# Layer 3's keys, values and products: biases by TensorE, banks emptied by ScalarE, masking moved into layer 2's expert loop

## The chip, the cores and the metric

The kernel runs on one core of a Trainium2 chip. The metric is device time in microseconds (us): the median of several executions. A core has five engines that run their own instruction streams in order and wait for one another by semaphores: TensorE (PE in the rows; its weight loads are PEld), VectorE (DVE), ScalarE (ACT), GpSimd (POOL) and SyncE (SP, which here only starts DMA transfers).

## The reference

A model of four layers, each an attention and a feed-forward part, over `x` (8 batches of 256 tokens of 256 numbers) and a context `ctx_1024` of the same shape. The change touches two neighbouring parts.

Layer 2's feed-forward part is a mixture of 8 experts with 2 chosen for each token:

```python
logits = jnp.einsum('bsd,de->bse', x, Wg) + bg
probs = jax.nn.softmax(logits / TEMP, axis=-1)
vals, idx = jax.lax.top_k(probs, K)
...
h = jax.nn.gelu(jnp.einsum('bsd,edh->besh', x, W1) + b1[None, :, None, :], approximate=False)
out = jnp.einsum('besh,ehd->besd', h, W2) + b2[None, :, None, :]
y = jnp.einsum('bse,besd->bsd', gates, out)
```

Layer 3's attention has 16 heads of 16 numbers and no softmax; its keys and values come from the context alone, not from `x`:

```python
K = _split_heads(_linear(k, wk_w, wk_b))
V = _split_heads(_linear(v, wv_w, wv_b))
score = jnp.einsum('bhqd,bhkd->bhqk', Q, K) / dk
attn = jnp.where(mask, -jnp.inf, score)
ctx = jnp.einsum('bhqk,bhkd->bhqd', attn, V)
```

Without a softmax, the context product of a head is the query times the small matrix K^T V of that head.

## The kernel before, in words

The program is a row of stages, one after the other on each engine: `setup, l0, e0, p1, f1, p2, e2, x3, f3`. `e2` is layer 2's mixture of experts (class `Experts`; `e0` is layer 0's, the same class), `x3` layer 3's attention, `f3` its feed-forward part, `p2` layer 2's attention. Stages are parted by a fence at which each engine waits for the others. Nothing is scheduled by a planner: each engine's order is the order in which its method of the stage (`pe`, `dv`, `ac`, `po`, `sp`) issues.

What layer 3's attention needs of the context does not depend on `x`, so it is computed inside stage `e2`, through hooks that `Experts` calls on the objects in its tuple `beside`. For each batch b (8 of them):

- `keys_pe(b)`: TensorE multiplies the context of the batch (256 tokens, in `ctxT`) with `wk` into one PSUM bank and with `wv` into another, 8 float32 matmuls of 256 columns; the profile shows each float32 matmul as two instructions (L2044, x16 a batch);
- `keys_dv(b)`: VectorE adds the bias row and writes `Ks` and `Vs` to SBUF (L2078, 128x512, twice a batch);
- in `amid_pe(b)`: TensorE forms the product K^T V, two blocks of 128x128, in bank 6 (L2064, x8 in the profile);
- in `amid_dv(b)`: VectorE multiplies it with the block mask `blk` (heads of 16, and the factor 1/4) and writes `As[b]`, over the part of `ctxT` that is no longer needed (L2089).

Of stage `e2` itself these steps stand around it, in this order on TensorE: transposes of the normalised tokens (`Norm.pe`, L283), the gate's logits (L957, L962), one pair of matmuls that counts the tokens of each expert (L912, L913), a list of places (`slots_pe`, L936, 32 matmuls in four groups of 8), and then the expert loop over 39 tiles of 128 tokens: transpose (`turn_pe`, L982), up (`up_pe`, L997) and down (`down_pe`, L947). VectorE's routing between the logits and the end of the list is one chain (`select`, `route`, `slots_dv`, `listed_dv`). `slots_dv` builds `values`, whose second half is `inblk` times the lane number `pid` (L1113), and `onehot` (L1115, 32 instructions; after each 8 the semaphore `seated` lets TensorE's next group go). When the list is done, SP starts to load the expert weights (four buffers) and POOL gathers the tokens. TensorE's order before was:

```python
self.norm.pe(t, lambda g: self.logits_pe(t, g))
# keys_pe(0), the counting pair, keys_pe(1), slots_pe
for n in range(9):
    # amid_pe(n): product of batch n, then keys_pe(n + 2)
self.turn_pe(t, 0)
```

`step_dv(v, i)` is a hook that VectorE calls once for each tile i of the expert loop.

## Time and profile before

| | |
|---|---|
| Median of 3 runs | 1799.55 us (1798.6 to 1801.32) |
| The profiled execution: its own time | 1807.56 us |
| Its span in the trace | 1805.8 us |
| Mean TensorE clock granted | 0.941 of full |
| Busy: TensorE, VectorE, ScalarE, GpSimd | 87%, 59%, 50%, 22% of the span |
| Stage `e2` in the trace, from its fence | 1404 us to about 1632 us |

The table's clock is the mean over the span of what the chip granted TensorE; a stretch has either 1.00 (2.4 GHz) or 0.50 (1.2 GHz). Times of the trace count from the start of the span of that one execution, which was 8 us slower than the median; a difference worked out in it is subtracted from the median.

### The profile page before, as it was taken

How to read it: one execution, taken by the hardware profiler on the slowest of the kernel's cores; microseconds unless marked ns; L12 is line 12 of the kernel's file. 1: busy time of each engine (PE TensorE's matmuls, PEld its weight loads, DVE VectorE, ACT ScalarE, POOL GpSimd, SP SyncE). 2: the span in 40 equal slices, each digit the busy share in tenths (PEclk: the TensorE clock that was granted, in tenths of full speed). 3: DMA queues.
4: the chain of work that ended last, by engine and by line, in shares of the span. 5: the costliest groups of instructions: out<-in, count | busy, mean ns of one | idle time of the engine just before them, and what ended most of it. 6: DMA issues, size and time to landing. Idle time of an engine off the chain costs nothing.

```text
span 1805.8 us, 27818 instructions
## 1 busy us (share of the span) xinstructions
PE 1565.6 (87%) x9882; PEld 1188.7 (66%) x9890; DVE 1058.7 (59%) x2954; ACT 906.8 (50%) x2034; POOL 390.6 (22%) x488
## 2 busy tenths in 40 slices
PE   7999965999489999999858699999999689995566
PEld 5777645999357766667535666677766378994444
DVE  7767744111556667666567755555555644225887
ACT  4888831333156666666539455555555102333366
POOL 1000012222232333332240100000000115543734
PEclk9999977999799999999968899999999889997879
DMA  5000047998300000000000200000000149993001
GB/s 167 1 2 1 2 140 291 325 328 280 120 6 7 7 7 7 7 1 1 1 1 1 82 12 7 7 7 7 1 1 1 59 147 309 359 337 104 1 12 36
DMA packets 57496, 143.92 MB, mean 80 GB/s; under 512 B 8208, under 2 KB 35088, under 8 KB 51088
## 3 DMA queue, kind: packets, MB, share of 16 engines
q1 hardware_dynamic: 49296, 123.80, 19.5%
q0 software_dynamic: 5952, 16.26, 2.7%
q10 hardware_dynamic: 2112, 2.10, 0.4%
q8 instruction: 79, 1.29, 0.3%
q14 instruction: 57, 0.47, 0.1%
HBM read 127.72 MB, written 14.42 MB: 79 GB/s over the span
## 4 chain that ended last, share of the span: by engine, by line
PE 70%; DVE 16%; ACT 6%; issue 4%; POOL 3%; DMA 2%; POOLq 1%; SPq 0%; DVEq 0%; ACTq 0%
PE bank L997 8%; PE bank L1425 8%; PE bank L947 8%; PE bank L1479 7%; PE bank L1492 6%; PE bank L1466 5%; PE bank L1429 5%; PE bank L1409 3%; PE bank L669 3%; PE bank L1831 2%; PE bank L685 2%; PE bank L700 2%; ACT p1f L1547 1%; PE bank L2044 1%; PE bank L606 1%
## 5 line engine op out<-in xcount | busy, mean ns | idle before, releaser
L1676 DVE TENSOR_REDUCE small<-bank 128x1 f32<-128x512 f32 x128 | 82.4, 686 | 108.7 <-PE bank L1479 108.7
L1672 DVE CUSTOM_DVE_ANT_0 p1f<-bank,p1f 128x512 f32<-128x512 f32 x128 | 83.2, 687 | 80.9 <-PE bank L1479 80.9
L1550 ACT ACTIVATE p2f<-bank,small 128x512 f32<-128x512 f32 x128 | 86.9, 684 | 86.2 <-DVE small L1676 86.2
L399 POOL TENSOR_SCALAR rs<-mv 128x4 f32<-128x4 f32 x16 | 3.6, 226 | 569.8 <-DVEq L229 554.1
L741 ACT ACTIVATE l<-l,small 128x256 f32<-128x256 f32 x256 | 108.9, 502 | 32.5 <-DVE small L807 32.1
L1547 ACT ACTIVATE p1f<-p1f,small 128x512 f32<-128x512 f32 x128 | 91.2, 714 | 67.5 <-DVE small L1672 67.2
L1016 ACT ACTIVATE e2a<-bank,WB 128x128 f32<-128x128 f32 x156 | 44.6, 369 | 158.8 <-PE bank L997 99.7
L807 DVE CUSTOM_DVE_ANT_0 l<-bank,small 128x256 f32<-128x256 f32 x256 | 90.8, 421 | 13.4 <-PE bank L685 12.5
L1425 PE MATMUL bank<-WA,HT 128*128 128x256 f32 x384 | 94.1, 389 | 4.9 <-DVE p1f L1617 4.9
L1561 ACT ACTIVATE p2f<-bank 128x512 f32<-128x512 f32 x128 | 75.2, 598 | 40.5 <-PE bank L1466 39.0
L1016 ACT ACTIVATE e0a<-bank,WB 128x128 f32<-128x128 f32 x128 | 36.6, 368 | 96.6 <-PE bank L997 96.6
L206 POOL TENSOR_TENSOR small<-small,nhalf 128x8 f32<-128x8 f32 x48 | 80.3, 1672 | 4.0
L1561 ACT ACTIVATE p1f<-bank 128x512 f32<-128x512 f32 x128 | 74.1, 589 | 13.2 <-PE bank L1466 13.2
L1425 PEld LDWEIGHTS bank<-WA,HT 128*128 128x128 f32 x384 | 71.0, 195 | 14.7 <-DVE p1f L1617 5.6
L997 PEld LDWEIGHTS bank<-e2a,WB 128*128 128x128 f32 x624 | 75.6, 192 | 5.6 <-issue 3.7
L997 PE MATMUL bank<-e2a,WB 128*128 128x128 f32 x624 | 76.2, 275 | 2.9 <-DVE e2a L1191 2.9
L1466 PE MATMUL bank<-ident,p1f 128*128 128x128 f32 x512 | 75.0, 275 | 3.4 <-ACT p1f L1561 2.2
L1466 PEld LDWEIGHTS bank<-ident,p2f 128*128 128x128 f32 x512 | 60.8, 141 | 23.6 <-ACT p2f L1561 13.3
L1466 PEld LDWEIGHTS bank<-ident,p1f 128*128 128x128 f32 x512 | 59.8, 141 | 24.5 <-ACT p1f L1561 17.4
L1479 PE MATMUL bank<-p1f 64*128 64x512 f32 x256 | 73.1, 641 | 2.1 <-ACT p1f L1528 2.1
L1466 PE MATMUL bank<-ident,p2f 128*128 128x128 f32 x512 | 74.7, 275 | 0.0
L1479 PE MATMUL bank<-p2f 64*128 64x512 f32 x256 | 73.6, 641 | 1.1 <-ACT p2f L1550 1.1
(414 smaller groups left out, 3822.0 us busy)
## 6 DMA issues: line engine op xcount, KB each, us to landing
WB<-in_L2pack SPq DMA_DIRECT2D x39, 514.0 KB
WB<-in_L2pack SPq DMA_DIRECT2D x39, 512.0 KB
WB<-in_L0pack SPq DMA_DIRECT2D x16, 1028.0 KB
WB<-in_L0pack SPq DMA_DIRECT2D x16, 1024.0 KB
e0a<-in_L0pack SPq DMA_DIRECT2D x7, 1028.0 KB
e0a<-in_L0pack SPq DMA_DIRECT2D x7, 1024.0 KB
e2a<-given_y SPq DMA_DIRECT2D x8, 512.0 KB, 6.5
WB<-in_ctx ACTq DMA_DIRECT2D x4, 512.0 KB
```

What stands on the lines that cost most here:

```text
L741: ins = a.e.activation(P[:, h * 256:(h + 1) * 256], P[:, h * 256:(h + 1) * 256], ACT.Exp, scale=-1.0, bias=self.mx[:, m + h:m + h + 1])
L807: ins = v.e.tensor_tensor_reduce(P[:, h * 256:(h + 1) * 256], k.bank(x)[:, h * 256:(h + 1) * 256], self.causal[:, h, :], -1.0, 3.0e38, ALU ...
L947: ins = t.e.matmul(y[:, 0:256], self.gb[i % 2][:, c, :], w[:, self.n1 + c * 256:self.n1 + (c + 1) * 256], start=c == 0, stop=c == nf - 1)
L997: ins = t.e.matmul(bk[:, j * 128:(j + 1) * 128], w[:, c * ff + ft * 128:c * ff + ft * 128 + 128], self.xT[i % 2][:, c, :], start=c == 0, s ...
L1425: ins = t.e.matmul(bk[:, i * 256:(i + 1) * 256], x[:, c, i * 128:(i + 1) * 128], w[:, c, at], start=c == 0, stop=c == 1)
L1429: ins = t.e.matmul(bk[:, i * 256:(i + 1) * 256], w[:, c, hg * 256 + i * 128:hg * 256 + (i + 1) * 128], x[:, c, :], start=c == 0, stop=c == 1)
L1466: ins = t.e.transpose(T[:, j * 128:(j + 1) * 128], self.P[u % 4][:, j * 128:(j + 1) * 128], k.ident[:, :])
L1479: t.e.matmul(k.bank(i % 2), self.Q[g % 2][rows, c, a * 128:(a + 1) * 128], self.K[g % 2][rows, c, :], start=True, stop=True).then_inc(self ...
L1492: ins = t.e.matmul(k.bank(4)[64 * o:64 * o + 64, c * 256:c * 256 + 256], self.V[g % 2][:, j, h * 64:(h + 1) * 64], self.PT[n % 2][o][:, j, ...
L1547: ins = a.e.activation(P, P, ACT.Exp, scale=-1.0, bias=self.mx[:, m:m + 1], accum_out=self.sm[:, m:m + 1])
L1550: ins = a.e.activation(P, k.bank(x), ACT.Exp, bias=self.mx[:, m:m + 1], accum_out=self.sm[:, m:m + 1])
L1561: a.e.activation(self.PT[u // 4 % 2][o][:, :, h * 128:(h + 1) * 128], k.bank(2 + u % 2).rearrange("p (k n) -> p k n", k=4), ACT.Copy).then ...
```

## The change

Five things change, all but one within stage `e2`.

1. **Biases.** `split_po`, run by GpSimd in stage `p2`, splits the two bias rows into three bfloat16 parts (10 instructions on 3 partitions, with rows `big`, `mid`, `low`). `keys_pe` starts each of its four accumulation groups with a bfloat16 matmul of a 3-row matrix of ones with these parts (L2082 in the changed kernel, 256 columns): 4 more matmuls a batch, 32 in all.
2. **Banks.** ScalarE instead of VectorE empties the key and value banks (`keys_ac`, L2091) and the product's bank (`amid_ac`, L2122), as plain copies.
3. **Mask.** VectorE multiplies `As` with `blk` later, in SBUF, one batch in each of the expert loop's tiles 2 to 9 (`step_dv`, L2134).
4. **Order on TensorE.** `keys_pe(0)` goes ahead of the stage's transposes and writes banks 6 and 7; `amid_pe(n)` is now keys of batch n+1, then product of batch n; number 0 stands ahead of the counting pair, 1 to 3 between the pair and `slots_pe`, 4 to 7 behind it. A group of keys waits only for its own bank pair to be empty.
5. **`values`.** ScalarE instead of VectorE multiplies `inblk` by `pid`, in `e0` as in `e2` (L1018 for L1113); `slots_pe` waits for it (`laned`), and ScalarE for `inblk` (`parted`).

```diff
@@ Experts.pe
+        for other in self.beside:
+            other.lead_pe(t)
         self.norm.pe(t, lambda g: self.logits_pe(t, g))
         for other in self.beside:
-            other.first_pe(t)
+            other.amid_pe(t, 0)
         bk, n = k.bank(7), self.n
         t.wait_ge(self.routing, self.SELECTED)
         ...
-        for other in self.beside:
-            other.next_pe(t)
+        for n in range(1, 4):
+            for other in self.beside:
+                other.amid_pe(t, n)
         self.slots_pe(t)
-        for n in range(9):
+        for n in range(4, 8):
             for other in self.beside:
                 other.amid_pe(t, n)
@@ slots_pe
+            if n == 0:
+                t.wait_ge(self.laned, 1)
@@ Experts.ac
         a.e.activation(self.first_gelu, k.nhalf[:, 0:1], ACT.Gelu)
+        for n in range(2):
+            for other in self.beside:
+                other.amid_ac(a, n)
+        a.wait_ge(self.parted, 1)
+        a.e.activation(self.values[:, :, 1, :], self.inblk, ACT.Copy, scale=self.pid).then_inc(self.laned.sem, 1)
+        for n in range(2, 8):
+            for other in self.beside:
+                other.amid_ac(a, n)
@@ slots_dv
-        e.tensor_scalar(self.values[:, :, 1, :], self.inblk, self.pid, None, ALU.mult)
@@ Layer3Attention
+    def halves(self, b):
+        first = 6 if b == 0 else 0 if b % 2 else 2
+        return self.k.bank(first), self.k.bank(first + 1)
     def keys_pe(self, t, b):
         k, lo = self.k, b * 256
         t.wait_ge(*self.ready_w)
+        t.wait_ge(self.split, 1)
+        if b > 2:
+            t.wait_ge(self.kb, b - 1)
+            t.wait_ge(self.vb, b - 1)
+        for h, (bk, w, flag) in enumerate(zip(self.halves(b), (self.wk, self.wv), (self.km, self.vm))):
             for a in range(2):
+                o = bk[:, a * 256:(a + 1) * 256]
+                t.e.matmul(o, k.onesbb[0:3, :], self.parts[:, h * 256:(h + 1) * 256], start=True, stop=False)
                 for c in range(2):
+                    ins = t.e.matmul(o, k.ctxT[:, c, lo + a * 128:lo + (a + 1) * 128], w[:, c, :], start=False, stop=c == 1)
             ins.then_inc(flag.sem, 1)
+    def keys_ac(self, a, b):
+        for bk, dst, done, flag in zip(self.halves(b), (self.Ks, self.Vs), (self.km, self.vm), (self.kb, self.vb)):
+            a.wait_ge(done, b + 1)
+            a.wait_ge(self.am, b - 1)
+            a.e.activation(dst[b % 2], bk.rearrange("p (a n) -> p a n", a=2), ACT.Copy).then_inc(flag.sem, 1)
     def amid_pe(self, t, n):
+        if b + 1 < 8:
+            self.keys_pe(t, b + 1)
+        K, V = self.Ks[b % 2], self.Vs[b % 2]
+        t.wait_ge(self.kb, b + 1)
+        t.wait_ge(self.vb, b + 1)
+        t.wait_ge(self.ac6, b)
         ...
+        if b == 7:
+            t.wait_ge(self.ac6, 8)
+    def amid_ac(self, a, n):
+        b = n
+        if b + 1 < 8:
+            self.keys_ac(a, b + 1)
+        a.wait_ge(self.am, b + 1)
+        a.e.activation(self.As[b], self.k.bank(6)[:, 0:256], ACT.Copy).then_inc(self.ac6.sem, 1)
@@ step_dv
+        elif i < 10:
+            A = self.As[i - 2].rearrange("p (c n) -> p c n", c=2)
+            v.wait_ge(self.ac6, i - 1)
+            v.e.tensor_tensor(A, A, ... blk ..., ALU.mult).then_inc(self.ad.sem, 1)
```

What moves on the engines. In these rows a float32 matmul counts once; `e2a` is the stage's own arena (the normalised tokens, `Ks`, `Vs`, `values`), `WA` the weights of layer 3 and the bias parts, `onesbb` the ones.

TensorE at the start of stage `e2`; the last row of stage `p2` stands first. Before:

```order
L1409 MATMUL bank7<-WB 128x256 x8
L283 MATMUL bank0<-ident,e2a 128x128 x4
L283 MATMUL bank1<-ident,e2a 128x128 x4
L283 MATMUL bank2<-ident,e2a 128x128 x4
L283 MATMUL bank3<-ident,e2a 128x128 x4
L957 MATMUL bank4<-HT,gates 8x512 x2
```

Now:

```order
L1422 MATMUL bank7<-WB 128x256 x8
L2082 MATMUL bank6<-WA,onesbb 128x256
L2084 MATMUL bank6<-WA,ctxT 128x256 x2
...
L2082 MATMUL bank7<-WA,onesbb 128x256
L2084 MATMUL bank7<-WA,ctxT 128x256 x2
...
L283 MATMUL bank0<-ident,e2a 128x128 x4
L283 MATMUL bank1<-ident,e2a 128x128 x4
```

A whole group of keys and values, with its four bias matmuls, now stands between the fence and the first transpose.

TensorE from the last logits to the first work behind the list of places. Before:

```order
L962 MATMUL bank7<-ident,e2a 128x8 x8
L2044 MATMUL bank0<-WA,ctxT 128x256 x4
L2044 MATMUL bank1<-WA,ctxT 128x256 x4
L912 MATMUL bank7<-e2a,trib 128x256
L913 MATMUL bank7<-e2a,onesbb 128x256
L2044 MATMUL bank2<-WA,ctxT 128x256 x4
L2044 MATMUL bank3<-WA,ctxT 128x256 x4
L936 MATMUL bank5<-e2a,HT 128x78 x32
L2064 MATMUL bank6<-e2a 128x128 x4
```

Now:

```order
L968 MATMUL bank7<-ident,e2a 128x8 x8
L2082 MATMUL bank0<-WA,onesbb 128x256
L2084 MATMUL bank0<-WA,ctxT 128x256 x2
...
L2111 MATMUL bank6<-e2a 128x128 x4
L915 MATMUL bank7<-e2a,trib 128x256
L916 MATMUL bank7<-e2a,onesbb 128x256
L2082 MATMUL bank2<-WA,onesbb 128x256
L2084 MATMUL bank2<-WA,ctxT 128x256 x2
...
L942 MATMUL bank5<-e2a,HT 128x78 x32
```

Ahead of the counting pair one group of keys and one product stand where one group of keys stood; between the pair and the list three groups and three products stand where one group stood; behind the list three groups and four products are left of six and eight.

ScalarE from the exponential to the first Gelu of the loop. Before:

```order
L1006 ACTIVATE e2a<-e2a 128x128
L1007 ACT_TABLE_LOAD
L1007 ACTIVATE e2a<-nhalf 128x1
L1016 ACTIVATE e2a<-bank0,WB 128x128 x4
```

Now:

```order
L1012 ACTIVATE e2a<-e2a 128x128
L1013 ACT_TABLE_LOAD
L1013 ACTIVATE e2a<-nhalf 128x1
L2091 ACTIVATE e2a<-bank0 128x512
L2091 ACTIVATE e2a<-bank1 128x512
L2122 ACTIVATE ctxT<-bank6 128x256
...
L1018 ACTIVATE e2a<-e2a,small 128x32x39
...
L1030 ACTIVATE e2a<-bank0,WB 128x128 x4
```

Between them stand now 14 bank copies of 512 columns, 8 of 256, and the multiplication for `values` after the first two products. Two more copies of 512 (batch 0) stand ahead, behind the first copy of the transposed tokens (L383).

## Rows read from the trace of the kernel before

**Rows 1.** The page, busy time of each engine over the span.
```profile
PE 1565.6 (87%) x9882; PEld 1188.7 (66%) x9890; DVE 1058.7 (59%) x2954; ACT 906.8 (50%) x2034; POOL 390.6 (22%) x488
```

**Rows 2.** Busy time by stretch; after the engines TensorE's clock, DMA share, GB/s.
```profile
1445.41:1480.47 35.06, 31.12 (x161) 27.73 (x160) 18.33 (x45) 0.00 (x0) 3.03 (x3) 0.88 0.44 162
1505.08:1620.00 114.92, 114.92 (x802) 108.52 (x801) 33.59 (x72) 34.31 (x120) 63.58 (x61) 1.00 0.96 346
1406.25:1412.75 6.50, 5.61 (x19) 3.65 (x20) 5.76 (x17) 1.20 (x2) 3.27 (x5) 0.50 0.78 247
1437.00:1453.75 16.75, 8.23 (x49) 6.83 (x50) 15.40 (x63) 0.00 (x0) 3.03 (x3) 0.50 0.35 114
1445.40:1463.40 18.00, 15.10 (x70) 13.42 (x70) 11.38 (x33) 0.00 (x0) 3.03 (x3) 0.76 0.85 310
897.75:900.75 3.00, 3.00 (x16) 1.50 (x14) 0.00 (x0) 0.00 (x0) 0.00 (x0) 0.50 0.00 0
```

**Rows 3.** Timeline of TensorE: start, duration, what, idle time before it and releaser.
```profile
1407.14 3.65 PE L283 MATMUL bank<-ident,e2a 128*128 128x128 f32 x16 [5.25 <-DVE e2a L332]
...
1422.90 3.72 PE L2044 MATMUL bank<-WA,ctxT 128*128 128x256 f32 x16
1427.97 0.28 PE L912 MATMUL bank<-e2a,trib 128*128 128x256 bf16 x1 [1.35 <-DVE e2a L1067]
1428.09 0.27 PE L913 MATMUL bank<-e2a,onesbb 128*128 128x256 bf16 x1
1428.20 3.62 PE L2044 MATMUL bank<-WA,ctxT 128*128 128x256 f32 x16
1440.82 0.70 PE L936 MATMUL bank<-e2a,HT 128*128 128x78 bf16 x8 [9.00 <-DVE HT L1115]
...
1444.71 0.70 PE L936 MATMUL bank<-e2a,HT 128*128 128x78 bf16 x8 [0.60 <-DVE HT L1115]
...
1480.47 0.44 PE L982 MATMUL bank<-ident,e2a 128*128 128x128 f32 x2 [0.52 <-DVE ctxT L2089]
```

**Rows 4.** The chain that ended last, behind the list of places: start, duration, what.
```profile
1448.32 2.05 PE bank L2064 x8
1450.37 5.28 PE bank L2044 x16
1455.65 0.89 PE bank L2064 x8
1456.55 3.46 PE bank L2044 x16
```

**Rows 5.** Timeline of VectorE in the routing.
```profile
1434.14 0.42 DVE L1094 TENSOR_TENSOR e2a<-e2a 128x256 f32<-128x256 f32 x1
...
1438.92 0.54 DVE L1113 TENSOR_SCALAR e2a<-e2a,small 128x1248 bf16<-128x1248 bf16 x1
1439.37 5.29 DVE L1115 TENSOR_SCALAR HT<-e2a 128x128 bf16<-128x128 bf16 x32
...
1446.89 2.48 DVE L2078 TENSOR_TENSOR e2a<-bank,rows 128x512 f32<-128x512 f32 x4
```

**Rows 6.** Timeline of ScalarE in the same stage.
```profile
1408.35 0.60 ACT L383 ACTIVATE HT<-bank 128x512 f32<-128x512 f32 x1 [10.22 <-PE bank L283]
...
1483.58 1.14 ACT L1016 ACTIVATE e2a<-bank,WB 128x128 f32<-128x128 f32 x4 [57.51 <-PE bank L997]
```

**Rows 7.** The expert loop, timeline of VectorE and of TensorE.
```profile
1500.43 0.42 DVE L1191 COPY e2a<-bank 128x256 f32<-128x256 f32 x1
...
1501.32 1.95 PE L997 MATMUL bank<-e2a,WB 128*128 128x128 f32 x16
```

**Rows 8.** Timeline of TensorE at the end of stage p1, before the clock's 0.50 above.
```profile
895.68 1.14 PE L1466 MATMUL bank<-ident,p1f 128*128 128x128 f32 x8 [1.89 <-ACT p1f L1561]
```

**Rows 9.** Timeline of VectorE, layer 0's routing (stage e0).
```profile
277.16 0.32 DVE L1113 TENSOR_SCALAR e0a<-e0a,small 128x368 bf16<-128x368 bf16 x1
```

**Rows 10.** Timeline of GpSimd: the idle time is its whole stage p2 behind the norm.
```profile
1404.22 0.23 POOL L399 TENSOR_SCALAR rs<-mv 128x4 f32<-128x4 f32 x1 [381.04 <-DVEq L229]
```

More of the change, by code:

```diff
@@ L898, in __init__ @@
         self.routing = f("e_routing", 3)
+        self.parted, self.laned = f("e_parted", 1), f("e_laned", 1)
         self.xt_t, self.xt_d = f("e_xt_t", nt), f("e_xt_d", nt)
@@ L1017, in ac, with behind_ac @@
                                    bias=w[:, 2 * self.ff + ft:2 * self.ff + ft + 1]).then_inc(self.gel.sem, 1)
+    def behind_ac(self, a, g):
+        self.logits_ac(a, g)
+        for other in self.beside:
+            other.norm_ac(a, g)
     def over(self, x):
@@ L1148, in dv @@
         self.listed_dv(v)
-        for other in self.beside:
-            other.first_dv(v)
         self.worth(v)
-        for n in range(9):
-            for other in self.beside:
-                other.amid_dv(v, n)
         self.turn_dv(v, 0)
@@ L1716, in po @@
         self.norm.po(q)
+        if self.which == 2:
+            self.after_po(q)
         if self.which == 1:
@@ L1745, in ahead_sp, with lead_pe, norm_ac @@
         pass
-    def first_pe(self, t):
+    def lead_pe(self, t):
         pass
-    def next_pe(self, t):
-        pass
-    def first_dv(self, v):
+    def norm_ac(self, a, g):
         pass
@@ L1757, in amid_pe @@
         pass
-    def amid_dv(self, v, n):
+    def amid_ac(self, a, n):
         pass
@@ L2006, in __init__ @@
         self.kb, self.vb, self.qb = f("x3_kb", 8), f("x3_vb", 8), f("x3_qb", 8)
+        self.split, self.ac6 = f("x3_split", 1), f("x3_ac", 8)
         self.am, self.ad, self.cm, self.ca = f("x3_am", 8), f("x3_ad", 8), f("x3_cm", 8), f("x3_ca", 8)
@@ L2027, in weights, with splits, split_po @@
         (self.wq, self.wk, self.wv, self.wo), self.ready_w = W, ready
+    def splits(self, free):
+        self.big, self.mid, self.low, self.parts = (free[0:3, i * 256:(i + 1) * 256].bitcast(BF16) for i in range(4))
+        self.rest = free[0:3, 1024:1536]
+    def split_po(self, g):
+        k, e, rest = self.k, g.e, self.rest
+        at = ROWS["bk"][0]
+        both, one = k.rows[0:3, at:at + 512], k.ident[0:3, :]
+        g.chain(e.tensor_copy(self.big, both))
+        g.chain(e.tensor_tensor(rest, both, self.big, ALU.subtract))
+        g.chain(e.tensor_copy(self.mid, rest))
+        g.chain(e.tensor_tensor(rest, rest, self.mid, ALU.subtract))
+        g.chain(e.tensor_copy(self.low, rest))
+        for x, j in ((self.big, 0), (self.mid, 1), (self.low, 2)):
+            g.chain(e.tensor_scalar(x, x, one[:, j:j + 1], None, ALU.mult))
+        g.chain(e.tensor_tensor(self.mid, self.mid, self.low, ALU.add))
+        e.tensor_tensor(self.parts, self.big, self.mid, ALU.add).then_inc(self.split.sem, 1)
     def free(self, t, key):
@@ L2038, in keys_pe @@
         t.wait_ge(*self.ready_w)
-        for h, w, flag, was in ((0, self.wk, self.km, self.kb), (1, self.wv, self.vm, self.vb)):
-            bk = k.bank(2 * (b % 2) + h)
-            t.wait_ge(was, b - 1)
+        t.wait_ge(self.split, 1)
[3 more added lines that the diff above has]
+        for h, (bk, w, flag) in enumerate(zip(self.halves(b), (self.wk, self.wv), (self.km, self.vm))):
             for a in range(2):
+                o = bk[:, a * 256:(a + 1) * 256]
+                t.e.matmul(o, k.onesbb[0:3, :], self.parts[:, h * 256:(h + 1) * 256], start=True, stop=False)
@@ L2049, in first_pe, with lead_pe, norm_ac @@
+    def lead_pe(self, t):
         self.keys_pe(t, 0)
-    def next_pe(self, t):
-        self.keys_pe(t, 1)
+    def norm_ac(self, a, g):
+        if g == 0:
+            self.keys_ac(a, 0)
     def amid_pe(self, t, n):
         k, b = self.k, n
-        if b < 8:
-            K, V = self.Ks[b % 2], self.Vs[b % 2]
-            t.wait_ge(self.ad, b)
-            t.wait_ge(self.kb, b + 1)
-            t.wait_ge(self.vb, b + 1)
-            for c in range(2):
-                for a in range(2):
-                    ins = t.e.matmul(k.bank(6)[:, c * 128:(c + 1) * 128], K[:, a, c * 128:(c + 1) * 128], V[:, a, c * 128:(c + 1) * 128],
-                                     start=a == 0, stop=a == 1)
-            ins.then_inc(self.am.sem, 1)
-        if b + 2 < 8:
-            self.keys_pe(t, b + 2)
-        if b == 8:
-            t.wait_ge(self.ad, 8)
@@ L2072, in keys_dv @@
-    def keys_dv(self, v, b):
-        k = self.k
-        for h, dst, bias, done, flag in ((0, self.Ks, "bk", self.km, self.kb), (1, self.Vs, "bv", self.vm, self.vb)):
-            v.wait_ge(done, b + 1)
-            v.wait_ge(self.am, b - 1)
-            bk = k.bank(2 * (b % 2) + h)
-            v.e.tensor_tensor(dst[b % 2], bk.rearrange("p (a n) -> p a n", a=2),
-                              k.row(bias).rearrange("p (o n) -> p o n", o=1).to_broadcast([128, 2, 256]), ALU.add).then_inc(flag.sem, 1)
@@ new lines, in amid_pe, with amid_ac @@
+        K, V = self.Ks[b % 2], self.Vs[b % 2]
+        t.wait_ge(self.kb, b + 1)
+        t.wait_ge(self.vb, b + 1)
+        t.wait_ge(self.ac6, b)
+        for c in range(2):
+            for a in range(2):
+                ins = t.e.matmul(k.bank(6)[:, c * 128:(c + 1) * 128], K[:, a, c * 128:(c + 1) * 128], V[:, a, c * 128:(c + 1) * 128],
+                                 start=a == 0, stop=a == 1)
+        ins.then_inc(self.am.sem, 1)
+        if b == 7:
+            t.wait_ge(self.ac6, 8)
+    def amid_ac(self, a, n):
+        b = n
[3 more added lines that the diff above has]
+        a.e.activation(self.As[b], self.k.bank(6)[:, 0:256], ACT.Copy).then_inc(self.ac6.sem, 1)
@@ L2550, in build @@
         x3.places(e2.Y[1])
+        x3.splits(k.WA[:, 6144:8192])
+        p2.after_po = x3.split_po
         x3.next = f3
```

20 lines of the change are left out of this document (4 added, 16 removed).

## The prediction

> **What bounds the kernel now.** I read the page first: TensorE is busy 87% of the span, the others 59% and less [rows 1], so a change pays where TensorE waits or runs at the lower clock. Then, by stretches, stage e2, where nearly all of the change lies. Its expert loop is TensorE and nothing else: in 114.92 us of it TensorE is busy for all 114.92, at clock 1.00 [rows 2]. What stands ahead of the loop decides when it starts, and it is not full. In the timeline of TensorE [rows 3] the reader is to see four things. The transposes start at 1407.14, after 5.25 us of idling for VectorE's normalised rows, and the clock is down to 0.50 from 1406.25 to 1412.75 [rows 2]. Between the last logits (1422.90, where the first group of keys starts) and the counting pair at 1427.97 lie 5.0 us, set by VectorE's selection, in which one group of keys (3.72) and a wait of 1.35 stand. After the pair and a second group TensorE idles 9.00 us for VectorE's `onehot` (L1115), does the list of places in four bits until 1445.41 (the last bit starts at 1444.71 and takes 0.70), and the clock has again fallen to 0.50, from 1437 to 1453.75 [rows 2]. Behind the list come six groups of keys and eight products, and the loop's first transpose starts only at 1480.47: 35.06 us, of which TensorE is busy 31.12 [rows 2, 3]. The chain of waits there [rows 4] runs over TensorE's own work: a product 0.89, a group of keys 3.46, 4.35 us a batch at full clock, and the first pair of them 2.05 and 5.28 at the low clock. So the list waits for VectorE with TensorE empty, and then TensorE's backlog holds up the loop. The change moves three groups and three products across that line.
>
> **The change, part by part.**
>
> *One batch, with its biases.* A float32 group costs 3.46 from its start to the next start [rows 4]. The bias matmuls have 256 columns in bfloat16; the nearest rows are the counting pair, of the same shape and type: the second starts 0.12 after the first, and the float32 group behind it 0.11 after that [rows 3], so a switch from bfloat16 to float32 shows no extra there. I take 0.12 each, 0.48 a batch. Below, a bfloat16 matmul can't cost less than nothing; above, one standing alone lasts 0.28 [rows 3], which would be 1.12 a batch. I take 0.12, since in `keys_pe` it is in a stream, as L913 is. A batch is then 3.46 + 0.48 + 0.89 = 4.83 us.
>
> *Behind the list.* Three groups and four products: 3 x 4.83 + 0.89 = 15.4, plus the last product's tail (0.3) and the copy of bank 6, which TensorE still waits for (0.5; it was 0.52 with VectorE's multiplication [rows 3]): 16.2. It was 35.06. That is **-18.9 us**, of which about 2.9 is the low clock that no longer meets this work (2.05 + 5.28 against 0.89 + 3.46), and the rest is work that moved ahead.
>
> *Between the counting pair and the list.* Three batches, 14.5 us from 1428.20: TensorE is free for the list at 1442.7, and VectorE's last eight `onehot` rows were done at about 1444.66. VectorE no longer does L1113, whose place was 1438.92 to 1439.37, 0.45 us [rows 5], so they are done at 1444.2. The first three bits of the list then have 1.5 us at 1442.7 to 1444.2, the last one 0.70 behind it: the list ends at 1444.9 and not 1445.41, **-0.5**. Bounds: if every bit takes the 0.70 that it had at the low clock, one after the other, it ends at 1445.5 (+0.1); if they halve, at 1444.6 (-0.8). The work here is hidden under VectorE's chain up to 1442.7 + 1.5; every microsecond beyond that is paid in full.
>
> *ScalarE.* It idles 57.51 us from its last routing instruction to the first Gelu [rows 6]. A 512-column copy out of PSUM is 0.60 there [rows 6], so a batch costs it about 0.6 + 0.6 + 0.4 = 1.6 us in a batch of 4.83: it can't set the pace, and a product of batch b needs copies that were made one batch earlier. The multiplication for `values`, 1248 columns, is at most 1248/512 x 0.60 = 1.5 us and can start when L1113 did at the latest, 1438.92 [rows 5]: done by 1440.4, and the list begins at 1442.7. I cost it at nothing; its cover is 2.3 us. Queued behind it are the copies of group 3, wanted by the product that starts at about 1441.8. The Trainium skill ("ScalarE: Activation LUTs", Rules for kernel authors) says that a multiplication or a copy belongs on VectorE, which is up to about three times as fast in bfloat16. The rows agree in the ratio (L1113 took VectorE 0.54), and by the rule the change would lose some 1 us on `values`; by the idle time in rows 6 it loses none, because the slower engine has nothing else to do, and the chain that is relieved is VectorE's.
>
> *Start of the stage.* Group 0 now stands ahead of the transposes. The fence opens at about 1404.15 (GpSimd's first instruction behind it is at 1404.22 [rows 10]); the group takes 3.72 + 0.48 = 4.2, so the transposes start at 1408.3 and not 1407.14: +1.2. Against that, TensorE is then working through the stretch in which it idled and the clock fell: 5.61 busy us at 0.50 [rows 2] are at most 2.8 us longer than at 1.00; I take 2.6 from them. But it still idles 2.2 us before the group, from the end of stage p2 at 1401.9 to 1404.15. At the end of stage p1 an idle time of 1.89 us [rows 8] was followed by 3 us at clock 0.50, from 897.75 to 900.75 [rows 2]. I take it that the clock falls here too, for about as long, which costs half of 3.4, 1.7 us. Sum: +1.2 - 2.6 + 1.7 = **+0.3**. Ahead of the second logits ScalarE does two copies more (1.2 us), in time that TensorE uses for transposes.
>
> *Before the counting pair.* Group 1 and product 0 are 3.46 + 0.48 + 0.89 = 4.83 with 0.2 of tail, in the 5.0 us that VectorE's selection takes: **+0.1**.
>
> *Layer 0.* VectorE's chain there loses L1113, 0.32 with its overlap [rows 9]; **-0.2**.
>
> *The loop.* Eight multiplications of 128x256 in SBUF on VectorE; the same shape is 0.42 there [rows 5]. VectorE is mostly idle in the loop (33.59 busy of 114.92 [rows 2]). The one place with little room is behind the first weight sum (L2317): L1191 ends at 1500.85 and the matmuls that read it start at 1501.32 [rows 7], so 0.42 more leaves the wait a little positive, **+0.1**. Elsewhere the multiplication stands in idle time; without that cover it would be 8 x 0.42 = 3.4. VectorE's 16 bank copies (L2078, 2.48 for four [rows 5]) leave the stage, on its way from the list to the loop; TensorE's own work was the limit there, so they give nothing beyond the wait at 1446.89, which is in the 35.06.
>
> *GpSimd.* The ten instructions of the split run in 381 us in which it idles [rows 10]: nothing.
>
> Sum: -18.9 - 0.5 + 0.3 + 0.1 - 0.2 + 0.1 = -19.1. The profiled execution took 1807.56, and would take 1788.5; from the median, 1799.55 - 19.1 = **1780.5 us**.
>
> **The rivals.**
>
> *The clock doesn't fall at the start.* The Trainium skill ("TensorE: Matmul & The Clock Gate", Why this matters for your kernels) says to avoid idle gaps of more than about 3 us, and would let the 2.2 us pass. For it as a mechanism here: the wait of 1.35 us ahead of the counting pair [rows 3] left the clock up until 1437 [rows 2]. Against it: the 1.89 us at the end of p1 [rows 8], after which the clock was down [rows 2]. Then the 1.7 falls away: -20.8, 1778.8. A chance of 0.25.
>
> *The bias matmuls cost what they cost alone, 0.28.* Each is 0.16 dearer. Behind the list 12 x 0.16 = 1.9; ahead of the list another 12, of which the cover takes little, 1.6; 4 before the pair and 4 before the transposes, 0.6 each. Together 4.7: -14.4, 1785.2. For it: in `keys_pe` one stands between float32 matmuls on both sides, which no row shows. Against: the 0.11 behind L913. A chance of 0.12.
>
> *The loop waits for its weights.* They can only start when the list is done. Before, DMA was busy 0.85 of the 18 us from 1445.40 to 1463.40 [rows 2]; now the loop starts at about 1461.5, inside that. If the first tiles had to wait until 1463.4 it would cost 2.2: 1782.7; and as DMA is at 0.96 in the loop [rows 2], little of it would be caught up. Against: the first tile's weights are the first to land, and the rest are wanted tile by tile. 0.07.
>
> *The change doesn't do what it says*: a wait in ScalarE's queue (for `parted`, or for a product) holds TensorE so that the backlog stays behind the list. It would show as idle time before L942 or L2111; about 1799.5. For it I find nothing in the order of the two queues. 0.02.
>
> *Slower.* A bfloat16 matmul in the middle of float32 groups stalls TensorE. There are 32, nearly all on the path, so it decides from 19.1/32 = 0.6 us above the 0.12, at 0.7 each. At 0.9 the kernel would take 1799.55 - 19.1 + 32 x 0.78 = 1805.4. No row comes near. 0.03.
>
> **How the numbers follow.** The forecast has 0.45, the clock's rival 0.25, the dear biases 0.12, the weights 0.07, no effect 0.02, slower 0.03; 0.06 is left for a time under 1776, were the loop's own start-up or the stages behind it to gain as well. The predicted time is the forecast's, 1780.5. The range runs from 1775.5, which takes in the better bound of the list, the clock's rival and 2 us of spread between executions, to 1786.5, which takes in the dear biases. A measurement of this kernel can tell about 0.2% (3.6 us) from no change. Faster by more than that: 0.95; within it: 0.02; slower: 0.03.
>
> **What the profile would show.** In the changed kernel, from the end of the list to the first transpose of the loop, 16.2 us and not 35.06; a batch of keys and product at 4.83 us start to start (4.35 and a smaller bias would show as less, 5.5 as the dear biases); no idle time before the list beyond VectorE's last rows, and the clock at 1.00 from about 1412 until the loop ends; the transposes starting at 1408 to 1410; ScalarE busy some 14 us in what was its 57.51 us of idling; the loop again TensorE alone, without idle time. What would make it wrong: a batch above 5.5 us, an idle time of TensorE before L2111 or L942, the loop's first tiles waiting for DMA, or a clock that falls in the stretch that I take as full.

## The result, and the profile of the changed kernel

The changed kernel took 1795.26 us (median of 8 executions, 1790.88 to 1798.15), the kernel before 1802.36 in the same measurement (1798.6 to 1808.43). The ratio is 0.9947 with a 95% interval of 0.9932 to 0.9961, so the change is worth 9.5 us (7.0 to 12.3) and not the 19.1 that was predicted. Measured a second time, the ratio was 0.9933 (0.9918 to 0.9948). (The medians alone differ by 7.1, at the edge of that interval.) It is faster, as forecast, but outside the range. Of the 14.8 us between the predicted 1780.5 and the measured 1795.26, 2.8 are the kernel before itself: the prediction subtracted from its median of 1799.55, and beside the changed kernel it took 1802.36.

The page of the changed kernel gives the busy times over a span of 1793.2 us (its execution took 1795.06):

```profile
PE 1568.6 (87%) x9914; PEld 1184.7 (66%) x9922; DVE 1048.8 (58%) x2936; ACT 919.8 (51%) x2060; POOL 401.2 (22%) x498
```

They say little: against [rows 1] VectorE is busy 10 us less, ScalarE 13 us more and TensorE 3 us more. The stretches of stage e2 say more. The first row is the lead group of keys, the second what lies between the list and the loop, the third the beginning of the loop (columns as in [rows 2]):

```profile
1404.66:1409.65 4.99, 4.99 (x20) 3.21 (x21) 3.39 (x11) 0.00 (x0) 4.56 (x8) 1.00 0.71 195
1447.91:1467.99 20.08, 19.05 (x92) 13.25 (x92) 4.04 (x19) 5.11 (x10) 3.02 (x3) 1.00 0.75 279
1468.00:1582.90 114.90, 110.86 (x774) 103.95 (x775) 43.42 (x81) 33.69 (x119) 61.45 (x59) 1.00 0.89 317
```

The reader is to see the clock at 1.00 (2.4 GHz) in all three, and 20.08 us behind the list where the prediction had 16.2 and the kernel before 35.06 [rows 2]. (In the third, TensorE is busy for 110.86 us, because it holds the loop's start-up; the 114.9 us behind the loop's first transpose have 110.84 in the kernel before.) Why it is 20.08 stands in TensorE's timeline of the changed kernel:

```profile
1398.71 3.72 PE L1422 MATMUL bank<-WB 128*128 128x256 f32 x16 [0.70 <-ACT WB L1580]
1404.66 0.28 PE L2082 MATMUL bank<-WA,onesbb 3*128 3x256 bf16 x1 [2.23 <-DVEq L229]
1404.87 1.13 PE L2084 MATMUL bank<-WA,ctxT 128*128 128x256 f32 x4
1405.93 0.28 PE L2082 MATMUL bank<-WA,onesbb 3*128 3x256 bf16 x1
...
1409.65 1.91 PE L283 MATMUL bank<-ident,e2a 128*128 128x128 f32 x16
...
1428.53 0.27 PE L916 MATMUL bank<-e2a,onesbb 128*128 128x256 bf16 x1
1428.73 0.28 PE L2082 MATMUL bank<-WA,onesbb 3*128 3x256 bf16 x1
...
1446.57 1.34 PE L942 MATMUL bank<-e2a,HT 128*128 128x78 bf16 x32
1447.84 0.28 PE L2082 MATMUL bank<-WA,onesbb 3*128 3x256 bf16 x1
1448.04 1.13 PE L2084 MATMUL bank<-WA,ctxT 128*128 128x256 f32 x4
1449.11 0.28 PE L2082 MATMUL bank<-WA,onesbb 3*128 3x256 bf16 x1
...
1452.82 1.05 PE L2111 MATMUL bank<-e2a 128*128 128x128 f32 x8
1453.81 0.28 PE L2082 MATMUL bank<-WA,onesbb 3*128 3x256 bf16 x1
...
1466.39 1.13 PE L2111 MATMUL bank<-e2a 128*128 128x128 f32 x8 [0.56 <-ACT ctxT L2122]
1467.99 0.44 PE L988 MATMUL bank<-ident,e2a 128*128 128x128 f32 x2 [0.47 <-ACT ctxT L2122]
```

A quarter of a group (one bias matmul and two float32 ones, which the profile shows as four instructions) goes from 1447.84 to 1449.11: 1.27 us, where 3.46 / 4 = 0.865 of float32 leaves 0.405 for the bias, not 0.12. A batch is 1453.81 - 1447.84 = 5.97 and not 4.83. No wait is shown: TensorE reads as busy throughout. The hint is in the timeline of its weight loads, same kernel:

```profile
1448.04 0.73 PEld L2084 LDWEIGHTS bank<-WA,ctxT 128*128 128x128 f32 x4
1449.10 0.09 PEld L2082 LDWEIGHTS bank<-WA,onesbb 3*128 3x128 bf16 x1 [0.33 <-issue]
```

A weight load can run beside the matmul before it (in the kernel with 128 rows, below, it starts 0.2 us ahead of its own matmul). The load of the 3-row weights doesn't: no load runs for 0.33 us, it starts at 1449.10, and its own matmul starts 0.01 behind it. The list stands at 1446.57 with no wait before it: it is TensorE's own backlog that sets it now. VectorE's `onehot` was done at 1444.67, 1.9 us earlier, as its timeline shows:

```profile
1439.38 5.29 DVE L1133 TENSOR_SCALAR HT<-e2a 128x128 bf16<-128x128 bf16 x32
...
1447.94 0.20 DVE L1142 COPY e2a<-bank 128x39 f32<-128x39 f32 x1 [2.19 <-PE bank L942]
```

To compare profiles whose stages begin at different times, I measure stage e2 from one mark, the start of the last 16 matmuls of stage p2 (L1422 above, 1398.71; in the kernel before L1409 at 1398.18), to the loop's first transpose. Before: 1480.47 - 1398.18 = 82.3. Changed: 69.3. That is -13.0, where the steps of the prediction for this stretch add up to -19.0. Called **mark to loop** below.

### The profile page after: what moved, and what is told of

The parts are those of the page before. It is cut to its first block, busy times and chain, and to the rows that moved or that the text cites. A ratio compares the mean times of both kernels' runs of the same rounds, so it can differ in the third digit from the quotient of the medians.

```text
span 1793.2 us, 27910 instructions
## 1 busy us (share of the span) xinstructions
PE 1568.6 (87%) x9914; PEld 1184.7 (66%) x9922; DVE 1048.8 (58%) x2936; ACT 919.8 (51%) x2060; POOL 401.2 (22%) x498
## 4 chain that ended last, share of the span: by engine, by line
PE 71%; DVE 15%; ACT 6%; issue 3%; POOL 2%; DMA 2%; POOLq 1%; SPq 0%; DVEq 0%; ACTq 0%
PE bank L1003 8%; PE bank L1438 8%; PE bank L953 8%; PE bank L1492 7%; PE bank L1505 6%; PE bank L1479 5%; PE bank L1442 5%; PE bank L1422 3%; PE bank L669 3%; PE bank L2084 2%; PE bank L1843 2%; PE bank L685 2%; PE bank L700 2%; ACT p1f L1560 1%; PE bank L606 1%
## 5 line engine op out<-in xcount | busy, mean ns | idle before, releaser
L807 DVE CUSTOM_DVE_ANT_0 l<-bank,small 128x256 f32<-128x256 f32 x256 | 90.8, 420 | 13.4 <-PE bank L685 12.5
```

The lines of the kernel that those rows point to most:

```text
L807: ins = v.e.tensor_tensor_reduce(P[:, h * 256:(h + 1) * 256], k.bank(x)[:, h * 256:(h + 1) * 256], self.causal[:, h, :], -1.0, 3.0e38, ALU ...
```

## The experiments

**Which kernels, and why.** Two theories for the 0.405 were open. A: it is the number of rows (3 of 128), which keeps the weights from loading beside a running matmul. B: it is the change between float32 and bfloat16. The first four were measured on one chip, beside the kernel before (1807.27 there).

**All 128 rows.** `parts` is laid on 128 partitions and zeroed first; rows 0 to 2 hold what they held.

```diff
+        g.chain(e.memset(self.parts, 0.0))
...
-                t.e.matmul(o, k.onesbb[0:3, :], self.parts[:, h * 256:(h + 1) * 256], start=True, stop=False)
+                t.e.matmul(o, k.onesbb[:, :], self.parts[:, h * 256:(h + 1) * 256], start=True, stop=False)
```

> The bias matmul reads all 128 rows: `onesbb` whole, and `parts` on 128 partitions with zeros behind row 2. Type, columns and number stay. Theory A (in the changed kernel the weights of a matmul of 3 rows, and those of the one behind it, don't load beside a running matmul, which makes a bias matmul 0.405 us where the counting pair shows 0.11 to 0.12): a batch falls from 5.98 us start to start to 3.46 + 0.89 + 4 x 0.12 = 4.8, the weight load ahead of it shows no wait of its own, the list becomes VectorE's to set again (ends some 2.6 us earlier), three batches behind it give 3.4, the lead group 1.1: about 7 us faster than the changed kernel, some 16 faster than the kernel before. Theory B (the switch between float32 and bfloat16 costs, whatever the rows): the batch stays at 5.98 and the time within 1 us of the changed kernel's.

Measured: 1787.97 us, ratio 0.9898 (0.9880 to 0.9916), 18.4 us faster than before. TensorE's timeline of this kernel:

```profile
1443.10 0.27 PE L2084 MATMUL bank<-WA,onesbb 128*128 128x256 bf16 x1
1443.20 1.03 PE L2086 MATMUL bank<-WA,ctxT 128*128 128x256 f32 x4
1444.07 0.27 PE L2084 MATMUL bank<-WA,onesbb 128*128 128x256 bf16 x1
```

and its weight loads:

```profile
1443.86 0.10 PEld L2084 LDWEIGHTS bank<-WA,onesbb 128*128 128x128 bf16 x1
1444.07 0.73 PEld L2086 LDWEIGHTS bank<-WA,ctxT 128*128 128x128 f32 x4
```

A quarter is 0.97, a batch 4.79; the load now starts 0.2 us before its matmul and has no idle time ahead of it. Mark to loop is 61.2. Types, columns and counts are those of the changed kernel, so A stands and B falls. The zeros cost TensorE nothing: the bias is at 0.97 - 0.865 = 0.11, as the counting pair has it.

**One row, but float32.** The bias as `onesf` (1 row) times the bias row, so that no type changes within a group.

```diff
-                t.e.matmul(o, k.onesbb[0:3, :], self.parts[:, h * 256:(h + 1) * 256], start=True, stop=False)
+                at = ROWS["bk"][0] + h * 256
+                t.e.matmul(o, k.onesf[0:1, :], k.rows[0:1, at:at + 256], start=True, stop=False)
```

> The bias matmul is a float32 one of 1 row (ones times the bias row), so nothing in a group changes type and the rows stay few. A float32 matmul of 256 columns is 3.46 / 8 = 0.43 in the stream. Theory A (few rows cost the overlap of the weight loads, 0.29 a matmul): 0.72 each, a batch 3.46 + 0.89 + 4 x 0.72 = 7.2 us, 1.25 more than in the changed kernel; eight of them on the path make it some 10 us slower than the changed kernel, no faster than the kernel before. Theory B (the switch of type costs): 0.43 each without a switch, a batch 6.1, about 1 us slower than the changed kernel.

Measured: 1820.61 us, ratio 1.0077 (1.0060 to 1.0094), 13.9 us slower than before and some 24 slower than the changed kernel, more than A had it. A quarter of a group, in TensorE's timeline of this kernel (the bias is two instructions here):

```profile
1464.69 0.69 PE L2083 MATMUL bank<-rows,onesf 1*128 1x256 f32 x2
1465.31 1.13 PE L2085 MATMUL bank<-WA,ctxT 128*128 128x256 f32 x4
1466.37 0.69 PE L2083 MATMUL bank<-rows,onesf 1*128 1x256 f32 x2
```

1.68 a quarter, so 0.82 for a bias: 0.43 of its own and 0.39 on top, where A expected 0.29. The extra tenth seems to lie between its two instructions (they take 0.62 from start to start of what follows, where two of 128 rows take 0.43 and the change out of few rows 0.10); no run takes it apart further. With 0.82 a batch is 7.6 and eight of them 13 us longer than in the changed kernel. The rest, some 10 of the 22.8 us by which mark to loop grew (to 92.1), fits the clock: it fell twice for about 10 us each, and TensorE worked through both at half speed. By stretches of this kernel:

```profile
1406.50:1416.00 9.50, 9.50 (x26) 6.16 (x25) 1.54 (x6) 0.92 (x2) 2.55 (x5) 0.50 0.36 121
1420.00:1430.00 10.00, 9.66 (x44) 4.06 (x42) 2.98 (x9) 3.04 (x7) 0.00 (x0) 1.00 0.16 58
1430.50:1440.00 9.50, 9.50 (x23) 6.18 (x24) 2.29 (x9) 1.90 (x4) 0.00 (x0) 0.50 0.01 2
```

In the 10 us before the second fall TensorE was idle for 0.34 us; it had gone through transposes and logits and 2 us of such a group. Neither theory of the cost had foreseen either fall.

**No biases.** The first float32 matmul of each pair starts the sum instead; this kernel leaves the key and value biases out of its output.

```diff
-                t.e.matmul(o, k.onesbb[0:3, :], self.parts[:, h * 256:(h + 1) * 256], start=True, stop=False)
...
-                    ins = t.e.matmul(o, k.ctxT[:, c, lo + a * 128:lo + (a + 1) * 128], w[:, c, :], start=False, stop=c == 1)
+                    ins = t.e.matmul(o, k.ctxT[:, c, lo + a * 128:lo + (a + 1) * 128], w[:, c, :], start=c == 0, stop=c == 1)
```

> No bias matmuls: the key and value biases are left out of the output. It prices all 32 of them at once. A batch is 3.46 + 0.89 = 4.35 us. If the biases are all that my prediction mis-sized: lead group 1.6 less, list set by VectorE (about 2.6 less), three groups behind the list 4 x 0.405 each, 4.9 less: 9.1 us faster than the changed kernel, some 18.5 faster than before. If most of the miss lies elsewhere (the start of the stage, the product that waits for bank 6, the loop), it gains less than 5.

Measured: 1786.37 us, ratio 0.9893 (0.9873 to 0.9913). Mark to loop is 59.6, 9.7 less than in the changed kernel, and a batch is 4.35. That is the first branch of what was expected (9.1), not the one of less than 5: the 32 bias matmuls are what was mis-sized. Without them the kernel is 19.3 us faster than before, with 128 rows 18.4, which the intervals don't part.

**`values` back on VectorE.** The waits on `parted` and `laned` go with it.

```diff
-        a.e.activation(self.values[:, :, 1, :], self.inblk, ACT.Copy, scale=self.pid).then_inc(self.laned.sem, 1)
...
+        e.tensor_scalar(self.values[:, :, 1, :], self.inblk, self.pid, None, ALU.mult)
```

> `values` is multiplied by VectorE again, as in the kernel before, and ScalarE doesn't do it. Theory A (TensorE's three dear batches set when the list can start): VectorE is done 0.45 us later than 1444.58, the list's last wait is still TensorE's own work until 1446.57: no difference, within 0.5 us, but for layer 0, where 0.2 may come back. Rival (the list waits for VectorE or for ScalarE's `values`): 0.3 to 0.6 us slower, and an idle time before L942.

Measured: 1795.21 us, ratio 0.9936 (0.9919 to 0.9954), which is the changed kernel's. There is no idle time before the list. Mark to loop is 70.9, 1.6 more than in the changed kernel, and all 1.6 lie in the lead group (6.58 us from 1404.81 to the transposes, against 4.99), where this execution's clock fell; the stretch in this kernel's profile:

```profile
1407.00:1410.00 3.00, 3.00 (x8) 1.61 (x6) 2.07 (x7) 0.00 (x0) 2.83 (x5) 0.50 0.91 270
```

So this move is worth nothing as long as TensorE's three batches take longer than VectorE's chain. With 128 rows, where the list waits for VectorE again, it was not measured.

**Few rows, but next to each other.** This kernel and the next three were measured on another chip (the kernel before: 1805.43). Each bank's bias is one matmul over 512 columns, both ahead of the group's float32 matmuls.

```diff
+        for h, bk in enumerate(self.halves(b)):
+            t.e.matmul(bk, k.onesbb[0:3, :], self.parts[:, h * 256:(h + 1) * 256].rearrange("p (o n) -> p o n", o=1).to_broadcast([3, 2, 256]),
+                       start=True, stop=False)
...
-                t.e.matmul(o, k.onesbb[0:3, :], self.parts[:, h * 256:(h + 1) * 256], start=True, stop=False)
```

> Each bank's bias is one matmul of 3 rows and 512 columns (the 256 bias values read twice), and both stand ahead of the group's eight float32 matmuls, 2 a batch and next to each other, instead of 4 spread over the group. If each change between 3 and 128 rows costs (into the few rows about 0.2, out of them about 0.1, as the timeline of the changed kernel has it: 1.27 a quarter against 0.865 + 0.11), a batch has one pair of changes instead of four: 3.46 + 0.89 + 2 x 0.21 + 0.3 = 5.1 us, and the time is within 2 us of the kernel whose bias matmuls have 128 rows. If each matmul of few rows costs, whatever stands beside it: two of them, 2 x (0.21 + 0.29), a batch of 5.35 us, about 3.5 us slower than with 128 rows.

Measured: 1789.39 us, ratio 0.9907 (0.9890 to 0.9923). TensorE's timeline of this kernel:

```profile
1444.66 0.60 PE L2080 MATMUL bank<-WA,onesbb 3*128 3x512 bf16 x2
1445.19 3.72 PE L2086 MATMUL bank<-WA,ctxT 128*128 128x256 f32 x16
1448.75 1.05 PE L2113 MATMUL bank<-e2a 128*128 128x128 f32 x8
1449.74 0.60 PE L2080 MATMUL bank<-WA,onesbb 3*128 3x512 bf16 x2
```

A batch is 5.08. Of that 3.46 + 0.89 are the float32 work and 2 x 0.21 the columns of the biases, which leaves 0.31 for one change into few rows and one out of them. Four such pairs at 0.29 make the 5.97 of the changed kernel. So the change of rows costs, not the matmul: 5.35 is excluded.

**The last product in a bank of its own.** 128 rows, and product 7 goes to bank 4.

```diff
-        t.wait_ge(self.ac6, b)
+        t.wait_ge(self.ac6, min(b, 6))
...
-                ins = t.e.matmul(k.bank(6)[:, c * 128:(c + 1) * 128], K[:, a, c * 128:(c + 1) * 128], V[:, a, c * 128:(c + 1) * 128],
+                ins = t.e.matmul(k.bank(4 if b == 7 else 6)[:, c * 128:(c + 1) * 128], K[:, a, c * 128:(c + 1) * 128], V[:, a, c * 128:(c + 1) * 128],
...
-            t.wait_ge(self.ac6, 8)
+            t.wait_ge(self.ac6, 7)
```

> Bias matmuls of 128 rows, and the last product goes to bank 4 instead of bank 6, so it doesn't wait for ScalarE's copy of the product before it, and the loop's first transpose waits for the copy of product 6 alone. In the changed kernel these waits are 0.56 and 0.47 us. Expected: both gone or nearly (the last product also needs ScalarE's copy of the last values, which may leave 0.1 to 0.3), the loop starts 0.7 to 1.0 us earlier behind the list than with one bank. Rival: the loop's start is set by ScalarE's or VectorE's work behind the products (the copy and the mask of the first block), and TensorE then waits 0.5 to 1.0 us there instead: no gain in the time.

Measured: 1786.99 us, ratio 0.9892 (0.9879 to 0.9905). Both waits are gone from TensorE's timeline of this kernel:

```profile
1460.70 2.07 PE L2113 MATMUL bank<-e2a 128*128 128x128 f32 x16
1462.61 0.38 PE L988 MATMUL bank<-ident,e2a 128*128 128x128 f32 x2
1463.67 2.02 PE L1003 MATMUL bank<-e2a,WB 128*128 128x128 f32 x16 [0.68 <-DVE e2a L1204]
```

Mark to loop is 59.9, 1.3 less than with one bank, and the wait behind the transpose stays at 0.68, so it isn't given back there. In the time itself 1.3 us is less than the measurement can tell. The kernel is faster than both given ones; measured beside the changed kernel on the same chip, it is at 0.9892 of the kernel before where that is at 0.9933, and the intervals don't meet.

**Without the lead group.** 128 rows; group 0 stands behind the logits and fills banks 2 and 3, and batch 0 stands behind the pair.

```diff
-        for other in self.beside:
-            other.lead_pe(t)
         self.norm.pe(t, lambda g: self.logits_pe(t, g))
         for other in self.beside:
-            other.amid_pe(t, 0)
+            other.lead_pe(t)
...
-        for n in range(1, 4):
+        for n in range(3):
...
-        for n in range(4, 8):
+        for n in range(3, 8):
```

> Bias matmuls of 128 rows, and the first group of keys stands behind the logits as in the kernel before, not ahead of the transposes; between the counting pair and the list stand three batches, behind it four and a product. It prices point `start of the stage`. Expected: TensorE idles some 5.2 us ahead of the transposes and works on them at the low clock (2.7 us lost), against 3.9 us for the lead group, of which 3.0 were idle: the logits end 1.8 us later. Behind the list one batch more, 4.8 us. Together 6.6 us slower than the kernel with 128 rows and the lead group, some 11.5 faster than before. Rival (the idle 2.2 us ahead of the lead group lower the clock just as often, so the lead group gains nothing at the start): 4.8 slower or less.

Measured: 1793.18 us, ratio 0.9929 (0.9916 to 0.9942), so 5.6 us (0.0031 of 1805) slower than with the lead group, on different chips; on the same chip it is 6.7 slower than the kernel with two banks, of which the bank is 1.3 by mark to loop. Mark to loop is 66.5, 5.3 longer. Behind the list are 4.8 of them, as expected. The start costs 0.5 and not 1.8: TensorE idles as expected, but the clock was down for some 3 us, not 6.5, and of TensorE's work it met only the first transposes (3.35 instead of 1.91), as its timeline shows:

```profile
1408.52 3.35 PE L283 MATMUL bank<-ident,e2a 128*128 128x128 f32 x16 [5.25 <-DVE e2a L332]
1411.80 1.88 PE L961 MATMUL bank<-HT,gates 128*8 128x512 f32 x4
```

**The changed kernel again.**

> The changed kernel once more, as it is. Expected: 0.995 of the kernel before, and a batch of 5.98 us. It shows whether the clock stays at 1.00 through the lead group in every profiled execution (as in the first one, where it never fell from 1380 to 1622) or falls in some after the idle 2.2 us, as I had taken it and as the kernel with `values` back on VectorE showed (groups of the lead batch at half speed from 1406.3 to 1410.2).

Measured: 1793.3 us, ratio 0.9933 (0.9918 to 0.9948), mark to loop 69.3, a batch 5.98. The clock did not fall in the stage in this execution either.

**How many rows are few?** The bias matmul reads 64, 127, 65 or 96 rows, zeros behind row 2.

```diff
-                t.e.matmul(o, k.onesbb[0:3, :], self.parts[:, h * 256:(h + 1) * 256], start=True, stop=False)
+                t.e.matmul(o, k.onesbb[0:64, :], self.parts[0:64, h * 256:(h + 1) * 256], start=True, stop=False)
```

> The bias matmul reads 64 of the 128 rows (rows 3 to 63 are zeros). If what costs is that a matmul and its neighbour read different numbers of rows, any number below 128 gives the batch of the changed kernel, 5.98 us, with the 0.33 us of the weight load's own wait. If it is few rows (up to 32, say a quarter of the array), 64 gives 4.79, as 128 do.

> The bias matmul reads 127 of the 128 rows. If any difference in the number of rows costs: a batch of 5.98 us. If the count is rounded up to some larger piece of the array, 127 is the same as 128: 4.79 us.

> 65 of 128 rows. 64 gave the batch of 5.98 us and 127 that of 4.80. If the count is rounded up to the whole array above half of it, 65 gives 4.8 as well. If it is rounded up to pieces of 32 rows, 65 takes 96 of them, which isn't the whole, and gives 5.98.

> 96 of 128 rows, to go with 65. Rounded up to the whole above a half: 4.8 us a batch. Rounded up to pieces of 32: 5.98, as with 65, since 96 is three pieces of four. 65 dear and 96 cheap, or the other way, would fit neither.

Measured, in one execution each: 1793.54 with 64 rows and 1785.73 with 127 (the kernel before: 1805.9), 1788.11 with 65 and 1787.68 with 96 (1804.24). The batch in TensorE's timeline, first for 64 rows,

```profile
1446.42 0.28 PE L2084 MATMUL bank<-WA,onesbb 64*128 64x256 bf16 x1
...
1452.40 0.28 PE L2084 MATMUL bank<-WA,onesbb 64*128 64x256 bf16 x1
```

then for 65 rows:

```profile
1444.30 0.27 PE L2084 MATMUL bank<-WA,onesbb 65*128 65x256 bf16 x1
...
1449.10 0.27 PE L2084 MATMUL bank<-WA,onesbb 65*128 65x256 bf16 x1
```

5.98 and 4.80; 96 and 127 rows give 4.80 as well. With 64 rows `parts` lies on 128 partitions with its zeros as it does with 65, so where it lies is not the cause. Half the array is the edge: with 3 and with 64 rows the neighbours of 128 rows pay, from 65 on they don't. The page "TensorEngine Tiling (Array Packing)" of the Trainium skill, under Key Properties, says that a change of tiling mode drains TensorE, and under Available Configurations it lists modes of 64 and of 32 rows beside those of 128. That a plain matmul of 64 rows or fewer runs in such a mode is a reading of mine; the traces fit it, in the edge (64 dear, 65 free) and in the drain (0.33 us without a weight load, ahead of the load). The price here is 0.29 to 0.31 us a pair of changes at full clock. The page "TensorE: Matmul & The Clock Gate" of the Trainium skill (Why this matters for your kernels) says that a single matmul of 32 rows takes as long as one of 128; the traces agree for the matmul itself (0.28 with 3 or 64 rows, 0.27 with 128), and show that the cost stands beside it, at its neighbours.

## Why the prediction was off, by its own steps

The stretch from mark to loop, cut where TensorE's timeline has marks of its own. Each number is a difference to the kernel before, in us; the last column is the kernel with 128 rows, which does the same work.

| Stretch | predicted | changed kernel | 128 rows |
|---|---|---|---|
| mark to the end of the logits | +0.3 | -0.9 | -1.9 |
| to the group behind the counting pair | +0.1 | +0.9 | 0.0 |
| to the end of the list | -0.5 | +2.0 | -0.7 |
| to the loop | -18.9 | -15.0 | -18.5 |
| sum | -19.0 | -13.0 | -21.1 |

(For example: from the list's end to the loop the kernel before has 35.06, the changed one 20.08, the one with 128 rows 1458.83 - 1442.29 = 16.54.)

**One batch, with its biases: the step that failed.** That "a switch from bfloat16 to float32 shows no extra there" and "I take 0.12 each" were read from the counting pair [rows 3]. Those two matmuls have 128 rows, the bias matmul has 3; I matched type and columns and took the shape as the same. The range's other end, 0.28 for one that stands alone, was too low too, because a matmul's own duration doesn't hold what its neighbours lose: in the changed kernel a bias matmul still lasts 0.28 and costs 0.405. The 0.29 on top, times 32, is 9.3 us; of these the kernel with 128 rows gets 8.1 back between mark and loop (69.3 to 61.2), for there the pair and the list wait for VectorE for 0.3 and 0.65 again. The rival "dear biases" had the right place and half of the price (0.16 each for 0.29); the rival "slower" had the right mechanism, a matmul that stalls its float32 neighbours, and would have decided only from 0.7 each, as the float32 row, at 0.82 and with two falls of the clock, did.

**Behind the list.** 16.2 was predicted, 20.08 came; three groups with four pairs each are 12 x 0.29 = 3.5 of the 3.9. The rest is of the size of a wait that I left out: product 7 waits for the copy of product 6 out of bank 6 (0.56 on `ac6`), in place of nothing in my sum. With the bias mended the step is right to 0.3 us (16.54).

**Before the counting pair.** Predicted +0.1, measured +0.9: product and group 1 take 5.97 with the dear biases, longer than the 5.0 us of VectorE's selection, and the pair, whose input VectorE had at 1427.64, starts only at 1428.42, behind the product. With 128 rows this is 0.0.

**Between the pair and the list.** "TensorE is free for the list at 1442.7" had 1.5 us to spare; three batches at 5.97 took 3.4 us more than three at 4.83 and the cover was gone, so the list ends 2.0 later instead of 0.5 earlier. With 128 rows the list waits 0.65 for VectorE again, as predicted, and ends 0.7 earlier. `values` on ScalarE (bound 1.5) was hidden as costed, and moving it back changed nothing. ScalarE's timeline of the changed kernel:

```profile
1437.90 1.34 ACT L1018 ACTIVATE e2a<-e2a,small 128x1248 bf16<-128x1248 bf16 x1 [2.70 <-DVE e2a L1128]
```

That is 2.5 times VectorE's 0.54 [rows 5]. The rule that the prediction cites there from the Trainium skill ("ScalarE: Activation LUTs", Rules for kernel authors) names multiplication and not copies; here neither cost the path anything by being slow.

**Start of the stage.** Predicted +0.3, with the clock falling in the 2.2 us before the lead group and 1.7 us paid for it. In two executions of the changed kernel it didn't fall; in the one with `values` back it fell 1.7 us after TensorE had resumed, for 1.6 us of loss. In the profiled executions of the nine other kernels with a lead group the idle time is the same 2.2 us, and the clock fell only in the one with a float32 row, whose work behind the gap is another. So that rival (0.25) was the likelier case, worth 1.7 us (the 3.4 halved there is the whole fall at the end of p1 in the trace, of which [rows 2] shows 3.00); without the 1.7 the start is -1.4 by my own numbers, and the kernel with 128 rows shows -1.9. The rule on idle gaps that the prediction weighed from the Trainium skill ("TensorE: Matmul & The Clock Gate") would let this gap pass; the traces agree in ten of twelve executions.

**ScalarE, GpSimd, the loop, layer 0.** Right. ScalarE waited for TensorE between its copies (0.60 each, as costed) and held it nowhere new but for bank 6. The split took GpSimd 12 us where it idled. The loop, from its first transpose to the first one of stage x3, takes 169.8 us and took 169.7: +0.1, and 169.7 to 169.8 in every other kernel here but the one with 127 rows. Layer 0's list came 0.2 us sooner.

**From the stage to the time.** The profiled executions differ by 1807.56 - 1795.06 = 12.5, the medians by 7.1 in the first measurement; the kernel before was profiled in an execution 5 us above its median. Executions of one kernel differ by up to 7 us, and with them the mean clock (the changed kernel: 1790.88 at 0.950, 1797.66 at 0.946); in the profiles of all kernels with a change the mark itself lies anywhere from 1395.4 to 1402.7, behind nearly the same work. So the table is the surer account of what the change did in the stage, and 0.9933 to 0.9947 of what it is worth. One gap stays open. In seven of nine measured comparisons the time moved by 2.7 to 4.1 us less in the change's favour than mark to loop did (with 128 rows 18.4 against 21.1, without biases 19.3 against 22.7), though the stretches from the loop on are alike to 1.2 us. The 82.3 of the kernel before rest on one profiled execution, in which the clock was down twice in the stretch; whether its usual execution takes some 3 us less there, no run shows. That the kernel with 128 rows comes out at 18.4, close to the 19.1 predicted, is therefore in part luck: its start was 2.2 us better than my step, and this gap took it back.

## What to carry to other kernels

A matmul of few rows (3 and 64 were measured) between matmuls of 128 costs about 0.3 us beyond its place in the stream, and no wait of TensorE shows it, only the weight load that no longer runs ahead: pad such operands with zeros to 65 rows or more, which was free here, or put the few-row matmuls next to each other. When the price of an instruction is read from a row, every part of its shape must match, rows as well as columns and type, and it is to be read as start to start of what stands around it, not as its duration. And a stretch that is hidden by 1.5 us is to be priced for what happens if it grows by twice that.

## What the runs showed of the hardware

- The edge at half the array: 3 rows 5.97 us a batch and 64 rows 5.98; 65, 96 and 127 rows 4.80, 128 rows 4.79.
- A float32 matmul of one row pays more: 0.82 us where one of 128 rows takes 0.43, so 0.39 on top against 0.29 for a bfloat16 one of 3 rows.
- The clock fell to half (1.2 GHz) in the middle of work that the profile shows as busy: with the float32 row at 1430, after 0.34 us of idle time in 10 us, for 10 us. In the changed kernel, whose few-row matmuls are bfloat16, it didn't fall from there to the loop in either execution. What makes the difference isn't shown.
- In the one execution with 127 rows it fell at the loop's start, for some 3 us behind the waits for bank 6 (0.56 and 0.47), and the first up matmuls took 3.57 us where the other kernels have 2.02; its loop took 171.3. TensorE's timeline of that kernel:

```profile
1457.77 3.57 PE L1003 MATMUL bank<-e2a,WB 128*128 128x128 f32 x16 [0.68 <-DVE e2a L1204]
```
